# A two-layer language tower on one core: the second layer's shared expert computed with stationary weights over chunks of 512 tokens, partly during routing, and routed rows scattered instead of gathered

## The reference, cut to what matters

```
h = h + attention0(layernorm(h))
h = h + experts0(layernorm(h))        # top 1 of 8, hidden width 512
h = h + relu_attention1(layernorm(h))
h = h + experts1(layernorm(h))        # top 2 of 8 and shared, hidden width 384

def experts1(x):                      # x: 4096 x 192
    scores = softmax(x @ w_router.T)
    e1, e2 = the two largest of scores + expert_bias
    w1, w2 = their scores, divided by their sum (+ 1e-9)
    out = w1 * swiglu(x, e1) + w2 * swiglu(x, e2) + swiglu(x, shared)

def swiglu(x, e):
    return (silu(x @ Wg[e].T) * (x @ Wu[e].T)) @ Wd[e].T
```

## Time and profile before

| what | value |
|---|---|
| runs | 1856.14, 1856.51, 1859.09 us; median 1856.51 |
| span of the profiled execution, first to last instruction | 1887.3 us |
| device time of the profiled execution itself | not recorded; only its span is |
| mean granted TensorE clock | 0.900 |
| second layer's router | 1398.8 to 1453.0 |
| second layer's experts: lead, routed pairs, tail | 27.6, 275.5, 131.2 us |
| first layer's routed pairs | 192.4 us |

### The profile page before, as it was taken

How to read it: one execution, slowest core, us unless ns; L and a number is a source line. 1 busy time by engine, 2 the same in 40 slices (tenths; PEclk the granted TensorE clock), 3 DMA queues, 4 the chain that set the end, 5 groups by cost and what they waited for, 6 DMA issues and landing times. The chain is left out here.

```text
span 1887.3 us, 29208 instructions
## 1 busy us (share of the span) xinstructions
PE 1636.2 (87%) x9188; PEld 911.1 (48%) x9189; DVE 1113.2 (59%) x2488; ACT 618.9 (33%) x840; POOL 404.1 (21%) x510
## 2 busy tenths in 40 slices
PE   5759998999899998767999658997867999999877
PEld 2411332333233331765666425666856666666555
DVE  5858997899799880464333264554567333333356
ACT  3401666666566677111111111110110112211111
POOL 6540000000000000002333273000110344443453
PEclk9865999999899999676999978998865999999989
DMA  2471222022122200710111120000610111112132
GB/s 82 142 136 15 35 35 34 14 36 35 18 34 34 35 1 3 227 42 17 42 42 42 48 58 14 2 2 29 179 34 5 32 50 56 50 51 49 50 89 71
DMA packets 66031, 92.82 MB, mean 49 GB/s; under 512 B 10065, under 2 KB 51604, under 8 KB 64916
## 3 DMA queue, kind: packets, MB, share of 16 engines
q1 hardware_dynamic: 53472, 66.66, 15.4%
q0 software_dynamic: 11520, 23.61, 4.8%
q10 hardware_dynamic: 960, 1.57, 0.5%
HBM read 61.82 MB, written 29.98 MB: 49 GB/s over the span
## 5 line engine op out<-in xcount | busy, mean ns | idle before, releaser
L502 DVE TENSOR_REDUCE sa_half_max<-psum 128x1 f32<-128x512 f32 x768 | 494.5, 687 | 80.9 <-PE psum L605 60.7
L559 ACT ACTIVATE sa_probs<-psum 128x1024 f32<-128x1024 f32 x384 | 372.3, 1022 | 169.3 <-PE psum L596 167.8
L605 PE MATMUL psum<-k_stack,q_stack 96*128 96x512 bf16 x768 | 285.9, 411 | 31.1 <-PEq L396 18.7
L596 PE MATMUL psum<-q_stack,k_stack 97*128 97x512 bf16 x768 | 231.6, 385 | 6.2 <-ACT sa_probs L559 5.4
L1379 PE MATMUL psum<-w_e_up_a,ex_xt 128*128 (+1 forms) x576 | 215.2, 516 | 0.0
L605 PEld LDWEIGHTS psum<-k_stack,q_stack 96*128 96x128 bf16 x768 | 75.1, 98 | 286.2 <-issue 152.5
L628 PE MATMUL psum<-sa_probs,sa_v_ext 128*32 128x512 f32 x1536 | 206.6, 610 | 0.6 <-ACT sa_probs L559 0.6
L1242 ACT ACTIVATE ex_silu<-psum 128x384 f32<-128x384 f32 (+1 forms) x144 | 74.6, 520 | 388.7 <-PE psum L1379 338.8
L1395 PE MATMUL psum<-w_e_down,ex_g_t 128*128 (+1 forms) x944 | 173.7, 335 | 2.0 <-DVE ex_g_t L1270 1.6
L1395 PEld LDWEIGHTS psum<-w_e_down,ex_g_t 128*128 128x128 f32 x944 | 151.9, 190 | 46.2 <-issue 44.5
L1263 DVE TENSOR_TENSOR ex_g<-ex_silu,psum 128x384 f32<-128x384 f32 (+1 forms) x144 | 84.6, 591 | 138.9 <-PE psum L1379 126.8
(11 more groups left out here) (244 smaller groups left out, 2034.7 us busy)
## 6 DMA issues: line engine op xcount, KB each, us to landing
y_rows<-ex_y SPq DMA_DIRECT2D x56, 192.0 KB, 2.0
q_stack<-qk_parts SPq DMA_DIRECT2D x66, 128.0 KB
k_stack<-qk_parts SPq DMA_DIRECT2D x66, 128.0 KB
qk_parts<-ep_parts SPq DMA_DIRECT2D x16, 384.0 KB
x_tokens<-x SPq DMA_DIRECT2D x16, 384.0 KB
qk_parts<-ep_parts SPq DMA_DIRECT2D x16, 192.0 KB
w_e_down<-e_down SPq DMA_DIRECT2D x1, 3072.0 KB
out<-h SPq DMA_DIRECT2D x8, 384.0 KB
```

The source lines that it names most:

```text
L502: nc.vector.tensor_reduce(half_max[:, g, hd, qt, half:half + 1], slot, AX.X, ALU.max).then_inc(ring_free[r], 1)
L559: nc.scalar.activation(probs[:, st % 2, 2 * pair:2 * pair + 2, :], ps[:, 2 * pair:2 * pair + 2, :], ACT.Exp, scale=SCALE0).then_inc(exp_do ...
L596: last = nc.tensor.matmul(ps[:, hd, :], kst[:, g, hd, kt * P:(kt + 1) * P], qst[:, g, hd, half * HALF:(half + 1) * HALF], start=True, stop ...
L605: last = nc.tensor.matmul(ps[:, 4 + r, :], qst[0:SK, g, hd, qt * P:(qt + 1) * P], kst[0:SK, g, hd, half * 512:(half + 1) * 512], start=Tru ...
```

## The change

- **Shared expert.** Its 16 pairs are taken out of the pipeline of `experts`. It is computed in 24 units: 8 chunks of 512 tokens by 3 parts of 128 hidden columns. Gate and up take the weights as the stationary side and turned tokens as the moving one, so their result is already turned and goes into the down product directly. The turned tokens are kept for all 4096 tokens in `s.shared.xt`: `close_attention` writes them there, and the copy of x (`keep`) goes.
- **Where the units stand.** Two chunks (6 units) during the second layer's `route`, with ScalarE copying the up part out of PSUM and GpSimd doing the products and the adds to `h`; there TensorE takes the ranks after the second unit and the table in three portions after the last three, with 16 table buffers in place of 4. One chunk ahead of the routed pairs, five behind them, with VectorE doing the products and adds.
- **Routed rows.** The table holds row numbers, from which `route` makes `slot_tokens` (source of the gather) and `slot_rows` (target of the scatter). y is written to its own row of `y_rows` by two indirect DMAs per pair on GpSimd, each in wait of the one before; empty slots go to 128 spare rows behind. In both layers the rows are read back by plain loads on SyncE, and the 64 and 32 gathers and `s.place` go.
- **Mixing.** By chunks of 512 tokens, with one multiply-add per tile, in bursts of two chunks.
- `close_attention` of the second layer is unrolled on TensorE.

```diff
 START = 1
+CHUNKS = NT // CT
+SHARED_IN_ROUTE = 2
+SHARED_AHEAD = 3
 @contextmanager
...
+        def x2_cols(u, k, w, rows_of=slice(0, P), j=0, n=CHUNK):
+            if layer == 0:
+                return x2_t[rows_of, u, w, j:j + n]
+            first = k * S + (u * CHUNK + j)
+            return s.shared.xt[rows_of, w, slice(first, first + n) if isinstance(k, int) else bass.ds(first, n)]
...
+    def __init__(self, sb, new_sem):
+        self.xt = sb("xt", [P, 2, T])
+        self.silu = sb("silu", [P, 2, CHUNK])
+        self.up = sb("up", [P, 2, CHUNK])
+        self.g = sb("g", [P, 2, CHUNK])
+        self.y = sb("y", [P, CT * D])
+        (self.gate_ps, self.up_ps, self.silu_done, self.up_left, self.g_done, self.down_done, self.y_copied,
+         self.y_added) = (new_sem("sh_" + n) for n in (
+             "gate_ps", "up_ps", "silu", "up_left", "g", "down", "y_copied", "y_added"))
...
+def shared_up(nc, pe, s, n):
+    sh, ps = s.shared, s.psum
+    chunk, f = divmod(n, sh.PARTS)
+    gate, up = ps[:, sh.PS_GATE + n % 2, :], ps[:, sh.PS_UP + n % 2, :]
+    x = [sh.xt[:, w, chunk * CHUNK:(chunk + 1) * CHUNK] for w in range(2)]
+    cols = slice(f * P, (f + 1) * P)
+    LOW, HIGH = slice(0, DB), slice(DB, P)
+    pe.wait_ge(sh.g_done, START + n - 1 if n else START)
+    nc.tensor.matmul(gate, s.up_a[:, 0, E, cols], x[0], start=True, stop=False)
+    nc.tensor.matmul(up, s.up_a[:, 1, E, cols], x[1], start=True, stop=False)
+    nc.tensor.matmul(gate, s.up_b[HIGH, E, cols], x[1][HIGH], start=False, stop=True).then_inc(sh.gate_ps, 1)
+    nc.tensor.matmul(up, s.up_b[LOW, E, cols], x[0][LOW], start=False, stop=True).then_inc(sh.up_ps, 1)
+def shared_down(nc, pe, s, n):
+    sh, ps = s.shared, s.psum
+    chunk, f = divmod(n, sh.PARTS)
+    if f == 0:
+        pe.wait_ge(sh.y_copied, START + 2 * chunk)
+    pe.wait_ge(sh.g_done, START + n + 1)
+    for j in range(CT):
+        last = nc.tensor.matmul(ps[:, sh.PS_Y + j // 2, j % 2 * D:(j % 2 + 1) * D], sh.g[:, n % 2, j * P:(j + 1) * P],
+                                s.down[:, E, f, :], start=(f == 0 and j % 2 == 0), stop=(f == sh.PARTS - 1),
+                                skip_group_check=True)
+    last.then_inc(sh.down_done, 1)
+def shared_silu(nc, act, s, n):
+    sh, ps = s.shared, s.psum
+    act.wait_ge(sh.gate_ps, START + n + 1)
+    act.wait_ge(sh.g_done, START + n - 1 if n else START)
+    nc.scalar.activation(sh.silu[:, n % 2, :], ps[:, sh.PS_GATE + n % 2, :], ACT.Silu).then_inc(sh.silu_done, 1)
+def shared_product(nc, dve, s, n):
+    sh, ps = s.shared, s.psum
+    dve.wait_ge(sh.silu_done, START + n + 1)
+    dve.wait_ge(sh.up_ps, START + n + 1)
+    dve.wait_ge(sh.down_done, START + n - 1 if n else START)
+    nc.vector.tensor_tensor(sh.g[:, n % 2, :], sh.silu[:, n % 2, :], ps[:, sh.PS_UP + n % 2, :], ALU.mult
+                            ).then_inc(sh.g_done, 1)
+def shared_add(nc, dve, s, chunk):
+    sh, ps = s.shared, s.psum
+    dve.wait_ge(sh.down_done, START + sh.PARTS * (chunk + 1))
+    for half in range(2):
+        tiles = s.h[:, chunk * CT + 2 * half:chunk * CT + 2 * half + 2, :]
+        nc.vector.tensor_tensor(tiles, tiles, ps[:, sh.PS_Y + half, 0:2 * D].rearrange("p (t d) -> p t d", d=D),
+                                ALU.add).then_inc(sh.y_copied, 1)
...
+            def product(n):
+                sh = s.shared
+                pool.wait_ge(sh.silu_done, START + n + 1)
+                pool.wait_ge(sh.up_left, START + n + 1)
+                pool.wait_ge(sh.down_done, START + n - 1 if n else START)
+                nc.gpsimd.tensor_tensor(sh.g[:, n % 2, :], sh.silu[:, n % 2, :], sh.up[:, n % 2, :], ALU.mult
+                                        ).then_inc(sh.g_done, 1)
...
+            def ranks():
+                pe.wait_ge(m["ones"], START + 2)
+                pe.wait_ge(m["chosen"], START + k_top)
+                flat = chosen[:].rearrange("p k t e -> p (k t e)")
+                nc.tensor.matmul(ps[:, PS_RANKS, 0:KT * E], before_me[:], flat, start=True, stop=True)
+                nc.tensor.matmul(ps[:, PS_TOTALS, 0:KT * E], all_ones[:], flat, start=True, stop=True
+                                 ).then_inc(m["ranks"], 1)
+            def table(first, last):
+                for i in range(first, last):
+                    pe.wait_ge(m["table_row"], START + 2 * (i + 1))
+                    nc.tensor.matmul(ps[:, PS_TABLE, 0:NBLK], in_slot[:, i % TABLE_BUFS, :],
+                                     in_block[:, i % TABLE_BUFS, :], start=(i == 0), stop=(i == KT - 1)
+                                     ).then_inc(m["table"], 1)
+            if not shared_units:
+                ranks()
+                table(0, KT)
+            else:
+                pe.wait_ge(s.experts_loaded, START + 16 * s.n_expert_loads)
+                RANKS_AFTER = 1
+                done = 0
+                shared_up(nc, pe, s, 0)
+                for n in shared_units:
+                    if n + 1 < len(shared_units):
+                        shared_up(nc, pe, s, n + 1)
+                    shared_down(nc, pe, s, n)
+                    if n == RANKS_AFTER:
+                        ranks()
+                    elif n > RANKS_AFTER + 1:
+                        until = KT * (n - RANKS_AFTER - 1) // (len(shared_units) - RANKS_AFTER - 2)
+                        table(done, until)
+                        done = until
...
+            def leave_up(n):
+                sh = s.shared
+                act.wait_ge(sh.up_ps, START + n + 1)
+                act.wait_ge(sh.g_done, START + n - 1 if n else START)
+                nc.scalar.copy(sh.up[:, n % 2, :], ps[:, sh.PS_UP + n % 2, :]).then_inc(sh.up_left, 1)
+            def copy_y(chunk):
+                sh = s.shared
+                act.wait_ge(sh.down_done, START + sh.PARTS * (chunk + 1))
+                act.wait_ge(sh.y_added, START + chunk)
+                for half in range(2):
+                    nc.scalar.copy(sh.y[:, 2 * half * D:(2 * half + 2) * D], ps[:, sh.PS_Y + half, 0:2 * D]
+                                   ).then_inc(sh.y_copied, 1)
+            for n in shared_units:
+                shared_silu(nc, act, s, n)
+                leave_up(n)
+                if n and n % SharedExpert.PARTS == 0:
+                    copy_y(n // SharedExpert.PARTS - 1)
+            if shared_units:
+                copy_y(SHARED_IN_ROUTE - 1)
...
-            link(nc.vector.tensor_copy(token_f[:], token_i[:]))
+            link(nc.vector.tensor_copy(row_f[:], row_i[:]))
+            link(nc.vector.tensor_scalar(lane[:], row_f[:, 0:1], float(ROWS), None, ALU.add))
...
-            link(nc.vector.tensor_copy(s.owner[:, 0:NBLK + BEFORE], owner[:]))
+            link(nc.vector.tensor_reduce(owner[:], reached[:], AX.X, ALU.add))
+            link(nc.vector.tensor_scalar(owner[:], owner[:], float(E - 1), None, ALU.min))
+            nc.vector.tensor_copy(s.owner[:, 0:NBLK], owner[:])
             dve.wait_ge(m["table"], START + KT)
-            nc.vector.tensor_copy(s.slot_tokens[:, 0:NBLK], ps[:, 2, 0:NBLK])
+            link(nc.vector.tensor_scalar(empty[:], ps[:, PS_TABLE, 0:NBLK], 0.0, lane[:], ALU.is_equal, ALU.mult))
+            link(nc.vector.tensor_scalar(slot_row[:], ps[:, PS_TABLE, 0:NBLK], float(ROWS), None, ALU.add))
+            link(nc.vector.tensor_tensor(slot_row[:], slot_row[:], empty[:], ALU.add))
+            link(nc.vector.tensor_copy(s.slot_rows[:, 0:NBLK], slot_row[:]))
+            if layer == 1:
+                link(nc.vector.tensor_scalar(second[:], slot_row[:], float(T), -float(T), ALU.is_ge, ALU.mult))
+                link(nc.vector.tensor_tensor(slot_row[:], slot_row[:], second[:], ALU.add))
...
+            def fetch(k, scattered=None):
                 pool.wait_ge(x_ps, START + k)
                 take_tokens(k)
                 gather_x(k, 0)
+                if scattered is not None:
+                    scatter_y(scattered, 1)
                 pool.wait_ge(half_done, START + k)
                 own_weights(k, 0)
                 gather_x(k, 1)
                 own_weights(k, 1)
-            if layer == 1:
...
-                pool.wait_ge(stored, START + 16 * ROUTED)
-                for c in range(ROUNDS):
...
+            def scatter_y(k, u):
+                if u == 0:
+                    pool.wait_ge(y_done, START + 2 * (k + 1))
+                    if not isinstance(k, int) or k > 0:
+                        pool.wait_ge(y_scattered[1], 16 * k)
+                else:
+                    pool.wait_ge(y_scattered[0], 16 * (k + 1))
+                pool.nop(nofuse=True)
+                pool.indirect_dma_start(out=y_rows, out_offset=bass.IndirectOffsetOnAxis(
+                    ap=to_rows[:, u:u + 1], axis=0), in_=y[:, u, :], in_offset=None).then_inc(y_scattered[u], 16)
+            for u in range(2):
+                pool.wait_ge(s.x_saved[u], START + 16 * B)
+            pool.wait_ge(s.experts_loaded, START + 16 * s.n_expert_loads)
+            fetch(0)
```

(92 more changed lines are left out.)

329 lines of the change are left out of this document (140 added, 189 removed).

## The result

The changed kernel takes 1842.57 us in the median (1834.67 to 1849.49), the kernel before 1856.51; the ratio is 0.9917, with a 95% interval of 0.9892 to 0.9942. It is faster by 0.8%, 14 us, where the prediction had 45, and it lies 2.6 us above the upper end of the range. One of its seven runs, 2136.91 us at a granted clock of 0.72 where the others have 0.90 to 0.91, counts in that median but neither in the limits in brackets nor in the ratio. A second comparison gave 1843.92 against 1861.17, ratio 0.989 (0.9857 to 0.9924).

A forecast was written before the change was run, and what follows sets the result against it. The prediction took TensorE to bound the routed pairs, VectorE the router, and waits for late gathers the tail. Terms -60 - 6 + 11 + 5 + 6 - 1 = -45 from 1856.5 gave 1811.5 us, range 1790 to 1840.

The forecast's parts named there:

- Tail: Behind the last routed pair: 15 units of 512 tokens replace thirteen pairs, 71 us instead of 131, -60.
- Sum: All terms, made on the span of 1887.3 us, give -45; taken from the runs' median 1856.5, this gives 1811.5.
- First layer: First layer's router +1.0, first fetch +0.8, two uncovered scatters in a row at the end +4.5; together +6.
- Second layer's router: Late ranks +1.5, small VectorE operations +1.2, VectorE waiting behind GpSimd 8; together +11, bounds +1 and +20.
- Lead: Ahead of the routed pairs: three units replace three shared pairs, 21.7 us instead of 27.6, -6.
- attention: Start of the second layer's attention: gathers leave, a load comes, GpSimd's mixing moves; -1, bounds -5 and +4.
- close: Close of attention: GpSimd's eight copies go, but TensorE sets the pace; 0.
- Routed pairs: Second layer's routed pairs: no cost in the median, more pairs waiting late for x; +5, bounds 0 and +34.
- The ring: Routed pairs' chained scatters: two landings L and 1.9 us, 7.1 at L of 2.6, inside the 7.57 us period.
- Rivals B and C: Scatter chain binds mildly or router takes its upper end, 1826 to 1848, 0.15; landings of 3.9 us, 1883, 0.09.
- Rivals B to E: Mild scatter binding or costly router 0.15; slow scatters 0.09; nearly free locks, clock rising in router 0.12; late tail loads 0.04.
- E: Tail: mixes wait for their plain loads, 104 us in place of 71, time 1844; chance 0.04.

The follow-up runs named there:

- the second profile: The changed kernel, unchanged, profiled once more: span 1843.9 us, time 1843.92 us, ratio 0.989 to the kernel before.

## Why the prediction was wrong, step by step

- **Tail, -60; it was -33.** The step that failed. "The thirteen trailing ones take 131.2 us, though TensorE works only 102.6 of them [...] a tail bound by something else" is true of that execution alone. Two others of the same kernel have 103.5, with TensorE working 96: what bounds the old tail is TensorE's own work, 7.49 us a pair. The reading of the earlier trace rows was wrong as well, in that execution too: the product behind which TensorE waited stands behind no mix, and no mix waited for its rows. The new tail was right: 70.6 for 71, a unit 4.27, TensorE waiting under 0.4 us at any product. The fused mix takes 0.35, not 0.3, without cost.
- **Sum.** The prediction saw that its span lay 31 us above the median and spread this over all terms ("terms 1.6% smaller change the sum by 0.7"). It was concentrated: 27.6 of it stood in the one stage that the change removes. Three runs of 1856 to 1859 and a span of 1887 should have been a rival of its own: "the excess is in the tail", with -33 for that term and 1838 for the time. The long stalls of TensorE of which the earlier trace rows show one were the place to look.
- **First layer, +6; it was +13.** Router and first fetch +1.5 of +1.8; the two scatters 4.9 of 4.5. Missing is GpSimd's drain, 6.6, which the scatters put last on the block's path.
- **Second layer's router, +11; it was +8.9.** Stretches 7.0 of 8, ranks 0.35 of 1.5, small operations 1.5 of 1.2. Without the stretches TensorE's lateness would show.
- **Lead -8.3 for -6, attention -0.6 for -1, close 0.** Close to forecast. The lead ran at a mean granted clock of 0.80 and 0.86 in the two profiles. The second pair waits 1.6 us for its x as written (its period is 9.13 against 7.56), but that falls into the routed pairs' stage: without it the forecast of the lead was -7.6, beside -8.3.
- **Routed pairs, +4.8 for +5,** period 7.56, scatters landing in 2.3 to 2.4 us. The number came out partly by luck: 1.6 of it is the second pair's wait, which the forecast had in the lead, and one pair late in the stage takes 11.2 to 11.6 us in three profiles, its second gather issued 2.6 us late in the second profile for no reason that the trace shows. The ring behind the forecast was wrong: it has 0.3 us of room, not what 2L + 1.9 leaves. With it, Rivals B and C would have started at a landing of an estimated 2.7 us (2.4 and the 0.3). It didn't come up: the median landing is 2.4, and none of the second layer's in the tile's view of the first profile exceeds it.
- **Rivals B to E** didn't occur. E's loads need 10.6 us a chunk at the tail's old 74 GB/s; the new tail moves 138 in the mean and no mix waited.

With the tail at -33 and the drain at +6.6 the same sum gives -45 + 27 + 6.6 = -11, beside -14 and -17 measured.

## What to carry to other kernels

Hold the span of the one profiled execution against the runs before reading any stage from it; if it lies outside them, ask in which stage the excess stands, above all if it's the stage to be removed. A stage in which the bounding engine shows a few long idle stretches among many even periods (7.49 us) is a stage with accidents: forecast it by the even period. Before a stretch is laid to a wait, see whether the instruction named had itself been idle before it: here no mix had. And when a transfer's wait moves onto an engine's queue, write the ring through all that the queue holds behind it, and look at which engine ends the block, and with what.
